# A gated-delta-rule attention kernel with attention and experts: block-inverse levels on half of the columns, gate sums as three products

## The reference

```python
q, k = l2norm(silu(conv4(x @ Wq.T))), l2norm(silu(conv4(x @ Wk.T)))
v = silu(conv4(x @ Wv.T))
alpha = exp(-exp(A_log) * softplus(x @ Wa.T + dt_bias));  beta = 2 * sigmoid(x @ Wb.T)
# per token: S = alpha * (S - beta * k (k.T S)) + k v.T ;  o = S.T q
x = x + rms_norm(o) @ Wo.T
x = x + layernorm(x) @ sign(W).T
x = x + causal_attention(layernorm(x))      # 16 heads of width 8, 4 key/value heads
x = x + experts(layernorm(x))               # 8 experts of width 512, the best 2 weighted
```

## Time and profile before

| | |
|---|---|
| median of 3 runs | 1836.87 us |
| lowest and highest run | 1832.37 and 1844.87 us |
| the profiled execution | 1827.64 us |
| its span, first to last instruction | 1825.9 us |
| its mean granted TensorE clock | 0.952 |
| TensorE, VectorE, ScalarE, GpSimd busy | 91%, 68%, 44%, 27% |

### The profile page before, as it was taken

The page is one execution under the profiler, slowest core; times in us unless marked ns, Lnnn a source line. Parts: engine busy times, 40 slices in busy tenths (PEclk is TensorE's granted clock), DMA queues, the critical chain, the costliest instruction groups (busy, mean ns, idle before and its releaser), DMA issues.

```text
span 1825.9 us, 32512 instructions
## 1 busy us (share of the span) xinstructions
PE 1657.6 (91%) x12563; PEld 999.0 (55%) x12563; DVE 1242.2 (68%) x2261; ACT 803.4 (44%) x1403; POOL 484.2 (27%) x986
## 2 busy tenths in 40 slices
PE   5778899999999999999999998898899899989998
PEld 1124666666665665666666666633455454544555
DVE  5947788888877878787767667555655764765443
ACT  5736456565556564555444444322233223323221
POOL 1023544535345354354435353000000000000000
PEclk9868899999999999899999999979999999999999
DMA  3000000000000000000000014000000000000000
GB/s 107 1 8 17 9 9 17 9 17 9 12 14 9 16 9 9 14 11 9 17 14 12 15 34 147 1 0 1 1 1 1 6 1 1 5 3 1 1 6 6
DMA packets 61338, 26.42 MB, mean 14 GB/s; under 512 B 54001, under 2 KB 57905, under 8 KB 60801
## 3 DMA queue, kind: packets, MB, share of 16 engines
q1 hardware_dynamic: 61184, 24.34, 5.2%
HBM read 16.40 MB, written 7.34 MB: 13 GB/s over the span
## 4 chain that ended last, share of the span: by engine, by line
PE 73%; DVE 13%; ACT 7%; issue 6%; SPq 1%; DMA 1%; POOL 0%; DVEq 0%; ACTq 0%
PE bank L795 6%; PE bank L779 6%; PE bank L501 6%; PE bank L782 6%; PE bank L535 4%; PE bank L592 4%; PE bank L481 3%; PE bank L524 3%; PE bank L451 3%; PE bank L483 3%; PE bank L619 2%; PE bank L742 2%; PE bank L431 2%; PE bank L421 2%; PE bank L545 2%
## 5 line engine op out<-in xcount | busy, mean ns | idle before, releaser
L1648 POOL TENSOR_TENSOR SU<-SU 128x28 f32<-128x28 f32 (+6 forms) x448 | 204.6, 457 | 35.1
L1271 DVE TENSOR_TENSOR AM<-bank,et 128x512 f32<-128x512 f32 x192 | 126.7, 688 | 126.8 <-PE bank L501 94.4
L1644 POOL TENSOR_TENSOR SU<-SU 128x28 f32<-128x28 f32 (+6 forms) x448 | 198.9, 444 | 35.2
L978 ACT ACTIVATE et<-bank 128x512 f32<-128x512 f32 x192 | 114.8, 598 | 207.7 <-PE bank L483 182.8
L1623 POOL TENSOR_TENSOR st<-st,nh 128x4 f32<-128x4 f32 x16 | 16.6, 1035 | 559.3 <-DVE st L1175 535.7
L1198 DVE SCALAR_TENSOR_TENSOR vc<-vy,conv,vc 128x512 f32<-128x512 f32 x192 | 148.8, 775 | 6.4 <-ACT vc L926 1.9
L795 PEld LDWEIGHTS bank<-WQ,AM 128*128 128x128 f32 x1024 | 129.2, 192 | 32.4 <-issue 24.9
L795 PE MATMUL bank<-WQ,AM 128*128 128x128 f32 x1024 | 138.0, 279 | 3.6 <-DVE X L1521 3.6
L779 PE MATMUL bank<-xnT,KQ 128*128 128x512 f32 x256 | 136.7, 616 | 0.0
L782 PE MATMUL bank<-xnT,KQ 128*128 128x512 f32 x256 | 132.5, 600 | 2.1 <-DVE AM L1511 2.1
L1640 POOL MEMSET SU<- 128x32 f32 x32 | 5.0, 155 | 482.1 <-DMA SU<-scratch 482.1
(11 more groups left out here) (217 smaller groups left out, 3449.2 us busy)
## 6 DMA issues: line engine op xcount, KB each, us to landing
scratch<-AM SPq DMA_DIRECT2D x128, 48.0 KB, 1.8
SM<-SM SPq DMA_DIRECT2D x288, 2.0 KB
SU<-scratch SPq DMA_DIRECT2D x128, 32.0 KB
WQ<-in_wqkv_dram SPq DMA_DIRECT2D x1, 2048.0 KB, 8.8
KQ<-in_wg_dram SPq DMA_DIRECT2D x4, 512.0 KB, 8.3
KQ<-in_wu_dram SPq DMA_DIRECT2D x4, 512.0 KB, 9.0
WQ<-in_wd_dram SPq DMA_DIRECT2D x1, 2048.0 KB, 15.5
WQ<-in_wo_dram SPq DMA_DIRECT2D x1, 1024.0 KB, 9.4
```

Source lines behind the costliest of these rows:

```text
L978: e.activation(et[:, q % 2, :], bank[2][:, :], ACT.Exp).then_inc(s_exp, 1)
L1271: e.tensor_tensor(dst, bank[(3, 1)[hh]][:, :].rearrange("p (k t) -> p k t", k=2), et[:, q % 2, :].rearrange("p (k t) -> p k t", k=2), ALU. ...
L1644: e.tensor_tensor(tmp[:, :, 0:k, 0:15 - k], sub[:, :, 0:k, k:k + 1].to_broadcast([128, 2, k, 15 - k]), sub[:, :, k:k + 1, k + 1:16].to_bro ...
L1648: e.tensor_tensor(sub[:, :, 0:k, k + 1:16], sub[:, :, 0:k, k + 1:16], tmp[:, :, 0:k, 0:15 - k], ALU.subtract).then_inc(s_su, 1)
```

## The change

`inv_a` and `inv_b` stream only every other block of columns: in `inv_a` the even blocks of m = 16 (level 0) or 32 (level 1) columns, in `inv_b` the odd ones, each 32 columns of 64, with the output in the same columns of the bank. The weights stay. The product for XP at level 1 streams columns 0 to 31. VectorE's subtractions in `inv_y` run over the same half (256 of 512 elements per partition); `inv_p` still reads all of bank 4. `ksel` becomes two products of 16 weight columns for an even t, at rows 0 and 32 of the bank, and one for an odd t at row 64, with a narrower `sel`. Four products on idle data (bf16, 512 columns) are added once, in the start-up at t = 2, so that all of banks 4 and 7 has been written.

```diff
-        sel = sb("sel", [128, 78])
+        sel = sb("sel", [128, 30])
@@ ksel
-                rows, o = (bank[7][64:80, :], 16) if kq else (bank[7][0:64, :], 64)
...
-                e.matmul(rows, sel[:, 14 - 2 * i8:14 - 2 * i8 + o], squares_of(t), start=i8 == 0, stop=i8 == 7).then_inc(s_ksel, 1)
+                for o in ((64,) if kq else (0, 32)):
+                    ins = e.matmul(bank[7][o:o + 16, :], sel[:, 14 - 2 * i8:30 - 2 * i8], squares_of(t), start=i8 == 0, stop=i8 == 7)
+                ins.then_inc(s_ksel, 1)
@@ new helper
+            def half(a, lv, odd):
+
+                m = 16 << lv
+                return a.rearrange("p (x y t) -> p x y t", y=2, t=m)[:, :, odd, :]
@@ inv_a
-                        ins = e.matmul(bank[4][pq, j * 64:j * 64 + 64], block_of(n, j, q, 64 * q), XP[pq, j, :],
-                                       start=True, stop=True)
+                        ins = e.matmul(half(bank[4][pq, j * 64:j * 64 + 64], lv, 0), block_of(n, j, q, 64 * q),
+                                       half(XP[pq, j, :], lv, 0), start=True, stop=True)
@@ inv_b
-                        ins = e.matmul(bank[5][pq, j * 64:j * 64 + 64], PP[pq, j, :], YP[pq, j, :], start=True, stop=True)
+                        ins = e.matmul(half(bank[5][pq, j * 64:j * 64 + 64], lv, 1), PP[pq, j, :], half(YP[pq, j, :], lv, 1),
+                                       start=True, stop=True)
                 if lv == 1:
                     for j in range(NJ):
-                        ins = e.matmul(bank[4][0:64, j * 64:j * 64 + 64], YP[0:64, j, :], PP[0:64, j, :],
+                        ins = e.matmul(bank[4][0:64, j * 64:j * 64 + 32], YP[0:64, j, :], PP[0:64, j, 0:32],
                                        start=True, stop=True)
@@ start-up, t == 2
                     e.wait_ge(s_set, NS_SET - 1)
+                    for o in (0, 32, 64):
+                        e.matmul(bank[7][o:o + 32, :], identb[:, 0:32], idle[:, :], start=True, stop=True)
+
+                    e.matmul(bank[4][:, :], identb[:, :], idle[:, :], start=True, stop=True)
@@ inv_y
-                e.tensor_tensor(YP[:, :, :], YP[:, :, :], wide(bank[5]), ALU.subtract).then_inc(s_iy, 1)
+                odd = lambda a: a.rearrange("p (j y t) -> p j y t", y=2, t=16 << lv)[:, :, 1, :]
+                y = odd(flat(YP[:, :, :]))
+                e.tensor_tensor(y, y, odd(bank[5][:, :]), ALU.subtract).then_inc(s_iy, 1)
...
-                    e.tensor_tensor(XP[0:64], XP[0:64], wide(bank[4])[0:64], ALU.subtract).then_inc(s_id, 1)
+                    e.tensor_tensor(XP[0:64, :, 0:32], XP[0:64, :, 0:32], wide(bank[4])[0:64, :, 0:32],
+                                    ALU.subtract).then_inc(s_id, 1)
```

More of the change, by code:

```diff
@@ L1702 @@
     lm[:, 0, :] = (s % 2 == 0) & (t[:, :64] == s % 64 + 1)
-    col = np.arange(78)[None, :] - 14 - s // 64
-    sel = ((col == 0) | (col == 32)).astype(f4)
+    sel = (np.arange(30)[None, :] - 14 == s // 64).astype(f4)
     wab = np.zeros((128, 96), f4)
```

## The result

The change made the kernel slightly slower where I forecast a gain: the median is 1847.24 us of 8 runs (1829.04 to 1859.86), before it 1833.71 us of 8 runs (1818.38 to 1844.87). The ratio is 1.0078 with a 95% interval of 1.004 to 1.0117. The forecast was 1817 us with a range of 1798 to 1845. The profiled execution of the changed kernel took 1829.04 us and is the fastest of its eight.

What follows compares the result with a forecast made beforehand. It took TensorE to bound the loop over head groups. Gains of 0 + 1.0 + 18.1 + 0.7 = 19.8 us, taken from the 1836.9 us median, gave 1817 us, range 1798 to 1845 us.

Steps and rivals of the forecast that it cites:

- What bounds the kernel: Loop over head groups: nearly every link of the chain that ended last is a TensorE line; gate sums hold 36.1 us.
- Part 1: Block inverse: halved streamed columns save TensorE 0 us, as weight loading sets the pitch; VectorE's halved subtractions gain 1 us.
- Part 2: Gate sums: three 16-column products overlap, 0.98 us instead of 1.97; 18.1 us gained in the loop, 0.7 in the start-up.
- The step that failed is the sum itself: Whole kernel: gains of 0 + 1.0 + 18.1 + 0.7 add to 19.8 us, giving 1817 us.
- rival 1: Loop, beside TensorE's idle time: clock falls more often; twelve more short stretches eat the gain, 1837 us; chance 0.11.
- Rival 2: Gate sums: quarters with 16 weight columns run one after another, +14 us, 1851 us; chance 0.05.
- rival 3: Block inverse: streamed columns do set the pitch, 68 us more gained, 1749 us; chance 0.08.
- rival 4: Loop: ScalarE's exponentials or VectorE's output step become the wait, half of the gate sums' gain lost, 1827 us; chance 0.12.
- The mean granted clock under 0.93: rival 1: Sign in the changed profile: mean clock still near 0.95 if right, under 0.93 if the clock falls more often.

Runs made afterwards that it cites:

- the inverse alone: Against the kernel before: inverse on half of the columns (TensorE and VectorE), gate sums as before; 1858.25 us beside 1827.43, ratio 1.016.
- the sums alone: Against the changed kernel: whole inverse as before, gate sums kept as three quarters; 1805.03 us beside 1827.43, ratio 0.9864 to before.
- one call on half: Against the changed kernel: only the second inv_b call's 16 products on half, other products on all columns; 1835.61 us, ratio 1.0018 to before.
- the filled runs: Idle products meant for waits, added to kernels with the second inv_b call (0.9888) or all calls (0.9817; loop's waits only 0.9896) on all columns.

## Why the prediction was wrong

- **What bounds the kernel** held in the main: TensorE's line is the chain, and most rounds with gate sums got 1.09 us shorter at the full clock, six of the eight that can be compared one to one.
- **Part 1, TensorE at the full clock, 0 us**: right, 0.06 us a round; VectorE did 26 us less work, and no run resolves whether 1 us of it reached the end (the inverse alone is 4 us lower without low time by the slope of 0.4, and anything from 4 us more to 10 us less is possible over the range of slopes). The rule of the Trainium skill, PSUM — Partial Sum Buffer, Specifications, that access patterns with gaps slow matmuls didn't show in the pitch: 1.05 us a group with gaps, 1.07 without.
- **Part 2, 18.1 + 0.7 us**: right. Six records in 0.97 us (0.98 forecast), and the sums alone save 18 us without low time and 22 us in the medians.
- **The step that failed is the sum itself**: it took the inverse's part as 0 us because its products take the same time, and left the clock to rival 1 with a chance of 0.11. Its missing term is some 100 us more of low time (277 against 176) at 0.4 us, 40 us. That the clock might fall was named, and the forecast gave it too little weight.
- **Rival 1 was mis-sized in two ways.** Its count of 12 was for added stretches of 3.4 us, 1.7 us each; in the changed profile four new stretches are 10 to 13.5 us long, and half of their length is 5 to 7 us each. And it placed them beside TensorE's idle time of 2.4 us; the new ones begin where TensorE is busy without a gap. The Trainium skill, TensorE: Matmul & The Clock Gate, What's actually happening, puts it as "the default state is throttled, and activity releases the throttle"; the runs agree, in that kernels whose products are equal in count and, at the full clock, in time kept 0.948 with 64 columns, 0.925 with 32 and 0.875 with 16, while the profile calls TensorE busy for 91, 91 and 92% of the span.
- Rival 2 (quarters one after another) and rival 3 (columns set the pitch) were wrong by the rows above; rival 4 (another wait) held in two of the eight rounds, where ScalarE's wait took the gain, and not in the six others.
- "The mean granted clock under 0.93: rival 1" was the right sign to look for: 0.925 over the runs.

## What to carry to other kernels

A saving that leaves TensorE's instructions in place and only thins what they stream is worth nothing at the full clock when the weight load sets the pitch, and can cost time through the granted clock (1.6% for the halved inverse alone); so read busy time and clock apart, and compare kernels by their time without low time and their low time. Keep the wide stream in the places where the lower stretches begin, even where half of it is thrown away. When a wait is to be filled, look in the new trace whether the filler stands in it before reading the time. Products with few weight columns belong in column quarters of one width next to each other: three took 0.97 us where two of unequal width took 1.97.

## What had not been expected of the hardware

The clock fell out of stretches in which the profile shows TensorE busy throughout at 1.0, as 3.30 of 3.30 us in the changed kernel and twice 3.20 of 3.20 us with one call on half. The same thinning was harmless in three calls of a round while the fourth was wide, and costly with the fourth thinned. And the answer to thinning is steep: 64, 32 and 16 columns gave some 187, 277 and 481 us of low time in kernels whose time without it is some 1735 to 1740 us. The version with the gate sums in quarters and the inverse as before is faster than both kernels (0.9864 of before); whether all columns with VectorE halved (0.9898) or one of the filled runs (0.9817) differs from it isn't decided.
